# State space convolution moved from VectorE to TensorE: four shifted projections with weights scaled by the taps

## The reference

```python
def _mamba(x, in_proj_w, conv_w, conv_b, x_proj_w, dt_proj_w, dt_proj_b, A_log, D, out_proj_w):
    xz = x @ in_proj_w.T
    xc, z = jnp.split(xz, 2, axis=-1)
    xt = jnp.pad(jnp.moveaxis(xc, 1, 2), ((0, 0), (0, 0), (D_CONV - 1, 0)))
    xt = conv(xt, conv_w, feature_group_count=D_INNER)      # 4 taps, one filter per channel
    xc = _silu(jnp.moveaxis(xt, 1, 2) + conv_b)
    x_dbl = xc @ x_proj_w.T
    dt = softplus(x_dbl[..., :DT_RANK] @ dt_proj_w.T + dt_proj_b)
    ...
    def step(h, ins):                                       # along the 256 rows
        dt_t, B_t, C_t, u_t = ins
        h = h * exp(dt_t[..., None] * A) + (dt_t * u_t)[..., None] * B_t[:, None, :]
        return h, einsum('bdn,bn->bd', h, C_t)
    ...
    y = y + D * xc
    return (y * _silu(z)) @ out_proj_w.T
```

## Time and profile before

| | us |
|---|---|
| median of 3 runs | 1524.51 (1522.3 to 1524.8) |
| the profiled execution | 1535.18 |
| its span in the trace | 1533.7 |

### The profile page before, as it was taken

The page is one execution under the profiler, slowest core; times in us unless marked ns, Lnnn a source line. Parts: engine busy times, 40 slices in busy tenths (PEclk is TensorE's granted clock), DMA queues, the critical chain, the costliest instruction groups (busy, mean ns, idle before and its releaser), DMA issues. The chain is left out here.

```text
span 1533.7 us, 31701 instructions
## 1 busy us (share of the span) xinstructions
PE 1304.3 (85%) x11784; PEld 805.7 (53%) x11784; DVE 1259.5 (82%) x3917; ACT 973.0 (63%) x1505; POOL 418.7 (27%) x316
## 2 busy tenths in 40 slices
PE   7999899998999988999958597678879789567746
PEld 4555566655665655666634484366347446323313
DVE  1355059999999998999999999998997787878983
ACT  6777778888786876878833353266677578434330
POOL 4110012232322213222222321222343343422450
PEclk9999999999998998999979799879979979678767
DMA  7878320333213320330005122104466356223320
GB/s 158 216 189 266 57 32 30 53 57 57 29 29 57 57 32 28 57 53 14 33 23 176 42 78 89 55 29 136 137 170 180 102 139 180 79 59 111 93 74 7
DMA packets 96856, 132.69 MB, mean 87 GB/s; under 512 B 20192, under 2 KB 80872, under 8 KB 93744
## 3 DMA queue, kind: packets, MB, share of 16 engines
q1 hardware_dynamic: 96688, 130.50, 33.6%
HBM read 124.95 MB, written 5.51 MB: 85 GB/s over the span
## 5 line engine op out<-in xcount | busy, mean ns | idle before, releaser
L1434 ACT ACTIVATE attn_arena<-ps 128x1024 f32<-128x1024 f32 x512 | 497.5, 1025 | 142.4 <-PE ps L456 139.6
L2066 DVE MATCH_REPLACE8 attn_late<-attn_shared,attn_late 128x256 f32<-128x256 f32 x1024 | 411.6, 410 | 0.0
L2063 DVE MAX8 attn_shared<-attn_late 128x8 f32<-128x256 f32 x1024 | 381.3, 415 | 11.9 <-ACT attn_late L1460 10.7
L456 PE MATMUL ps<-attn_arena 32*128 32x256 f32 x4096 | 343.0, 407 | 7.8 <-ACT attn_arena L1434 3.2
L470 PE MATMUL ps<-attn_arena 128*32 128x256 f32 x4096 | 279.0, 389 | 6.5 <-ACT attn_early L1442 3.0
L456 PEld LDWEIGHTS ps<-attn_arena 32*128 32x128 f32 x4096 | 231.4, 188 | 92.8 <-issue 65.4
L1297 POOL TENSOR_SCALAR attn_late<-attn_late 128x512 f32<-128x512 f32 x64 | 95.7, 1495 | 595.1 <-DVE attn_late L2066 595.1
L470 PEld LDWEIGHTS ps<-attn_arena 128*32 128x32 f32 x4096 | 109.2, 110 | 138.8 <-issue 63.1
L739 PE MATMUL ps<-attn_arena,attn_q 128*128 128x512 f32 x256 | 134.4, 660 | 15.0 <-DMA attn_arena<-ctxT 15.0
L1310 POOL TENSOR_TENSOR attn_late<-attn_late 128x1024 f32<-128x1024 f32 x48 | 113.2, 2362 | 121.5 <-DVE ps L1889 121.5
L761 PE MATMUL ps<-attn_arena 128*128 128x256 f32 x512 | 128.1, 396 | 0.0
(11 more groups left out here) (249 smaller groups left out, 1622.7 us busy)
## 6 DMA issues: line engine op xcount, KB each, us to landing
attn_arena<-ctxT SPq DMA_DIRECT2D x124, 256.0 KB, 4.7
attn_arena<-ctx SPq DMA_DIRECT2D x32, 512.0 KB, 4.2
attn_late<-rows SPq DMA_DIRECT2D x256, 64.0 KB, 2.3
attn_arena<-ctxV SPq DMA_DIRECT2D x15, 1024.0 KB, 13.0
attn_late<-maskT SPq DMA_DIRECT2D x20, 512.0 KB, 6.6
attn_late<-wide SPq DMA_DIRECT2D x64, 128.0 KB, 2.7
attn_early<-wide SPq DMA_DIRECT2D x64, 128.0 KB, 3.3
attn_arena<-maskT SPq DMA_DIRECT2D x12, 512.0 KB, 11.9
```

Of the source, the lines that this page charges most:

```text
L456: mm = pe.matmul(ps[:, first + j - 2 * i, u * S:(u + 1) * S], kx[n % 2][rows, k0:k0 + P], qpad[rows, n % GROUPS, b * S:(b + 1) * S], start ...
L1434: act.activation(probs[m % 2][:, 2 * i:2 * i + 2], ps[:, first:first + 2, :], ACT.Exp, scale=1.0 / 16.0).then_inc(exp_done, 1)
L2063: dve.max(top[:, t, turn], s[:, i, t] if turn == 0 else work[:, i, t]).then_inc(picked, 1)
L2066: dve.match_replace(work[:, i, t], top[:, t, turn], s[:, i, t] if turn == 0 else work[:, i, t], LOW).then_inc(picked, 1)
```

## The change

The convolution commutes with the projection: the sum over taps n of tap[c, n] times the projection of a shifted input is four projections of shifted inputs with weights scaled by the taps. `xT` gets three zero columns ahead of its 256, the taps are loaded as rows over all partitions into `wtap` (1 MB in place of the 8 KB of `cw`), and POOL multiplies them by the weights once, in step 49. PE then makes xc by four accumulating matmuls for each channel block (`make_xc`), in slot 1 of the step p-4, and z (`make_z`) in slot 2 behind it. ACT's `soften` reads the bank itself, with the bias, in slot 2, and Silu of z and `scale_input` follow in slot 3. DVE's `convolve`, ACT's copy to `xcp` and the semaphore `cv_ready` go. The size of a scratch area for dynamic DMAs is halved, which makes room for `wtap`.

```diff
-        xT = cut(early, 512, 2, S)
-        xcp = cut(early, 2560, C, S + TAPS - 1)
+        xT = cut(early, 512, 2, S + TAPS - 1)
+        xcd = cut(early, 2566, C, S)
+        wtap = sb("wtap", [P, 2, TAPS, C * P])
...
-            def make_xz(name, i):
+            def make_xc(i):
                 d = i % 2
-                if d == 0 and name == "xc":
+                if d == 0:
                     pe.wait_ge(misc_taken, misc["xs", i // 2] + 1)
-                    pe.wait_ge(ssm_loaded, SSM_LOADS)
-                begin(name, "ssm", i)
+                    pe.wait_ge(ssm_consts, 3)
+                    pe.wait_ge(ssm_zeroed, 3)
+                begin("xc", "ssm", i)
                 for k in range(C):
-                    m = k + (C if name == "z" else 0)
-                    mm = pe.matmul(M_[:, k * S:(k + 1) * S], win[:, d, m * P:(m + 1) * P], xT[:, d, :], start=True, stop=True)
+                    for n in range(TAPS):
+                        mm = pe.matmul(M_[:, k * S:(k + 1) * S], wtap[:, d, n, k * P:(k + 1) * P], xT[:, d, n:n + S], start=(n == 0), stop=(n == TAPS - 1))
+                mm.then_inc(misc_made, 1)
+
+            def make_z(i):
+                d = i % 2
+                begin("z", "ssm", i)
+                for k in range(C):
+                    mm = pe.matmul(M_[:, k * S:(k + 1) * S], win[:, d, (C + k) * P:(C + k + 1) * P], xT[:, d, TAPS - 1:], start=True, stop=True)
                 mm.then_inc(misc_made, 1)
...
                         for i in passes(-4, p):
-                            make_xz("z", i)
+                            make_xc(i)
...
                     if slot == 2:
+                        for i in passes(-4, p):
+                            make_z(i)
                         for i in passes(-2, p):
                             start_y(i)
...
                     if slot == 3:
-                        for i in passes(-5, p):
-                            make_xz("xc", i)
...
-            for w, name in ((nw, "nw"), (nb, "nb")):
+            for w, name in ((nw, "nw"), (nb, "nb"), (wtap.rearrange("p d n c -> p (d n c)"), "taps")):
                 sp.dma_start(w, a[name].partition_broadcast(P)).then_inc(ssm_loaded, 16)
...
+                    pool.wait_ge(ssm_loaded, SSM_LOADS)
+                    step(pool.tensor_tensor(wtap[:, 0], wtap[:, 0], win[:, 0, 0:C * P].unsqueeze(1).to_broadcast([P, TAPS, C * P]), ALU.mult))
+                    pool.tensor_tensor(wtap[:, 1], wtap[:, 1], win[:, 1, 0:C * P].unsqueeze(1).to_broadcast([P, TAPS, C * P]), ALU.mult).then_inc(ssm_consts, 1)
...
-                act.wait_ge(cv_ready, i + 1)
+                act.wait_ge(misc_made, misc["xc", "ssm", i] + 1)
                 if i:
                     act.wait_ge(du_ready, i)
-                act.activation(xcs, cvv, ACT.Silu).then_inc(u_ready, 1)
-                act.wait_ge(u_ready, i + 1)
+                act.activation(xcs[:, 0, :], M_[:, 0:S], ACT.Silu, bias=cb[:, d, 0:1])
+                act.activation(xcs[:, 1, :], M_[:, S:2 * S], ACT.Silu, bias=cb[:, d, 1:2]).then_inc(misc_taken, 1)
+                act.wait_ge(misc_taken, misc["xc", "ssm", i] + 1)
+                act.sem_inc(u_ready, 1)
+
+            def scale_input(i):
...
-                            take_misc(xcp[:, :, TAPS - 1:], M_.rearrange("p (c s) -> p c s", c=C), "xc", "ssm", i)
...
                         for i in passes(-4, p):
+                            soften(i)
+                    if slot == 3:
+                        for i in passes(-4, p):
                             act.wait_ge(misc_made, misc["z", "ssm", i] + 1)
                             if i >= 3:
                                 act.wait_ge(gated, i - 2)
                             act.activation(sz[i % 3], M_.rearrange("p (c s) -> p c s", c=C), ACT.Silu).then_inc(misc_taken, 1)
-                    if slot == 3:
-                        for i in passes(-4, p):
-                            soften(i)
+                            scale_input(i)
...
-            def convolve(i):
-                d = i % 2
-                dve.wait_ge(misc_taken, misc["xc", "ssm", i] + 1)
-                dve.wait_ge(ssm_zeroed, 3)
-                for k in range(C):
-                    tap = lambda n: xcp[:, k, n:n + S]
-                    step(dve.tensor_scalar(cvv[:, k, :], tap(TAPS - 1), cw[:, d, k, TAPS - 1:TAPS], cb[:, d, k:k + 1], ALU.mult, ALU.add))
-                    for n in range(TAPS - 1):
-                        ins = dve.scalar_tensor_tensor(out=cvv[:, k, :], in0=tap(n), scalar=cw[:, d, k, n:n + 1], in1=cvv[:, k, :], op0=ALU.mult, op1=ALU.add)
-                        if n < TAPS - 2 or k < C - 1:
-                            step(ins)
-                ins.then_inc(cv_ready, 1)
...
-                if turn == 4:
-                    for i in passes(-4, p):
-                        convolve(i)
...
-    nc = bacc.Bacc("TRN2", target_bir_lowering=False, num_devices=1)
+    nc = bacc.Bacc("TRN2", target_bir_lowering=False, num_devices=1, dynamic_dma_scratch_size=8192)
```

More of the change, by code:

```diff
@@ L246, in attention @@
         A = cut(arena, 23392, 2, 2 * 4, QUADS)
-        cw, cb = cut(arena, 23456, 2, C, TAPS), cut(arena, 23472, 2, C)
+        cb = cut(arena, 23472, 2, C)
         bdt, dcol = cut(arena, 23476, 2, C), cut(arena, 23480, 2, C)
@@ L253, in attention @@
         xs = cut(early, 0, T, E)
-        xT = cut(early, 512, 2, S)
-        gx = cut(early, 1024, 2, C, S)
-        xd = cut(early, 2048, 2, S)
-        xcp = cut(early, 2560, C, S + TAPS - 1)
+        xT = cut(early, 512, 2, S + TAPS - 1)
+        gx = cut(early, 1030, 2, C, S)
+        xd = cut(early, 2054, 2, S)
+        xcd = cut(early, 2566, C, S)
+        wtap = sb("wtap", [P, 2, TAPS, C * P])
         cvv = cut(early, 3078, C, S)
@@ L804, in start_y @@
                 pe.wait_ge(xcd_ready, i + 1)
-                pe.matmul(y_of(i), ident[:], xcp[:, :, TAPS - 1:], start=True, stop=False, skip_group_check=True).then_inc(y_started, 1)
+                pe.matmul(y_of(i), ident[:], xcd, start=True, stop=False, skip_group_check=True).then_inc(y_started, 1)
             def add_states(i, h):
@@ L1128, in _ @@
             sp.wait_ge(pv_done, CROSS_ITS)
-            for w, name in ((win, "win"), (wx, "wx"), (wout, "wout"), (alog, "alog"), (cw, "cw"), (cb, "cb"), (bdt, "bdt"), (dcol, "dcol")):
+            for w, name in ((win, "win"), (wx, "wx"), (wout, "wout"), (alog, "alog"), (cb, "cb"), (bdt, "bdt"), (dcol, "dcol")):
                 sp.dma_start(w, a[name]).then_inc(ssm_loaded, 16)
-            for w, name in ((nw, "nw"), (nb, "nb")):
+            for w, name in ((nw, "nw"), (nb, "nb"), (wtap.rearrange("p d n c -> p (d n c)"), "taps")):
                 sp.dma_start(w, a[name].partition_broadcast(P)).then_inc(ssm_loaded, 16)
@@ L1404, in _ @@
                     pool.tensor_tensor(xs, xs, nb.unsqueeze(1).to_broadcast([P, T, E]), ALU.add).then_inc(xs2_ready, 1)
[L1405 to L1407 removed]
+                if p == SSM_P[0] - 7:
+                    pool.memset(xT[:, :, 0:TAPS - 1], 0.0).then_inc(ssm_zeroed, 1)
                 if p == SSM_P[0]:
@@ L1546, in soften @@
                 d = i % 2
-                act.wait_ge(cv_ready, i + 1)
+                act.wait_ge(misc_made, misc["xc", "ssm", i] + 1)
                 if i:
                     act.wait_ge(du_ready, i)
-                act.activation(xcs, cvv, ACT.Silu).then_inc(u_ready, 1)
-                act.wait_ge(u_ready, i + 1)
+                act.activation(xcs[:, 0, :], M_[:, 0:S], ACT.Silu, bias=cb[:, d, 0:1])
[3 more added lines that the diff above has]
+            def scale_input(i):
+                d = i % 2
+                if i:
+                    act.wait_ge(y_started, i)
                 for k in range(C):
-                    ins = act.activation(xcp[:, k, TAPS - 1:], xcs[:, k, :], ACT.Identity, scale=dcol[:, d, k:k + 1])
+                    ins = act.activation(xcd[:, k, :], xcs[:, k, :], ACT.Identity, scale=dcol[:, d, k:k + 1])
                 ins.then_inc(xcd_ready, 1)
@@ L2136, in layouts @@
         "win": c(np.stack([w.T for w in both(i, "in_proj_w")], 1)),
-        "cw": c(np.stack([w.reshape(C, P, TAPS).transpose(1, 0, 2) for w in both(i, "conv_w")], 1)),
+        "taps": c(np.stack([w.reshape(C * P, TAPS).T for w in both(i, "conv_w")]).reshape(-1)),
         "wx": c(np.stack([np.concatenate([w[RANK:], w[:RANK]]).T.reshape(C, P, -1).transpose(1, 0, 2) for w in both(i, "x_proj_w")], 1)),
```

6 lines of the change are left out of this document (2 added, 4 removed).

## The result

The changed kernel takes **1545.74 us** (median of four runs, 1541.12 to 1551.22), the kernel before 1524.65 us (four runs, 1522.30 to 1526.53): a ratio of **1.0137, interval 1.0105 to 1.0169**, 21 us slower. The forecast was 1535, with 1505 to 1550 as its range. The direction is the forecast's; the size is twice its +10.7 us.

The account below looks back on a forecast made before the run. The bound was taken to change hands between VectorE and TensorE. Terms by step summed to +10.7 us on the profiled 1535.18 us, 1545.9, or 1535 us on the median's scale, with a range of 1505 to 1550.

Parts of the forecast that it names:

- Step 60: Pass 0: TensorE's added +2.5 us nearly covered by its 4.47 us wait for GpSimd; VectorE keeps its saving, -3.5 us.
- Steps 68, 80, 85 and 89: Router's logits, state sums, an FFN product and the output projection, each against VectorE's saving: +4.5, +2.1, -2.1, +1.9 us.
- Step 76: Two context score tiles end 3.5 us later, and VectorE's maximum follows: +2.4 us (0 to 2.5).
- The load: 1 MB of taps ahead of the context keys: 2.8 us at 375 GB/s, about half hidden; +1.5 us (0 to 3).
- Step 64: Context output projection starts 3.5 us later behind xc and z, so VectorE adds it late: +1.4 us (-1 to +3).
- Step 72: VectorE already waited 2.05 us for the context products, with TensorE full before: +2.5 us (0 to 2.5).
- Faster: VectorE stays the bound and bank 7 has slack: whole 31.9 us saving stays, 1494 us, half gives 1509; chance 0.20.
- No change: Context products, context scores and state sums cost nothing, router's logits 2 us: sum +1.2, or 1526 us; chance 0.14.
- A better clock: Added matmuls keep TensorE at 2.4 GHz, 13.8 us of lost time on the path: sum -3.1, 1521 us; chance 0.08.
- Worse: xc starts after a wait at 1.2 GHz, 3.7 us more in six passes: +22 more, 1557 us; chance 0.08.
- rival C: Set up for the follow-up runs: the load and ScalarE's work, laid bare, give VectorE's saving back; no chance given.

Follow-up runs that it names:

- z_four: Kernel before, each product of the z projection made four times over (12 added TensorE instructions a pass, slot 1 of p-4): 1536.32 us, ratio 1.0063.
- before_one_tap: Kernel before, VectorE applying one tap and leaving the other three out of the result: 1520.73 us, ratio 0.9951.
- one_tap: Changed kernel in its own order, only the last tap's product for xc, as many products as before: 1538.24 us, ratio 1.0065.
- z_first: Changed kernel with z projected before xc and copied out, bank 7 handed over at the old times, taps loaded late: 1539.15 us, ratio 1.0074.
- early_xc: Changed kernel with xc's 16 instructions at the old place, slot 3 of p-5, and z in slot 1 of p-4: 1546.45 us, ratio 1.0114.
- the square: Four variants of the change, over before: old handover with one or four products for xc, -0.3 and +12.0 us; late handover, +10.8 and +21.6.
- no_load: Changed kernel without the 1 MB load and GpSimd's two products, taps left out of the result: 1542.63 us, ratio 1.0103.

## Why the prediction was right in direction and wrong in size

The sum came to +10.7, and by the same steps the change costs +20.6. Step 60 makes 4.4 us of the difference, steps 48 and 76 make 2.7 each, steps 64 and 72 1.3 and 1.1.

**The mechanism held.** The removed work is worth little, since TensorE or ScalarE is late next; the saving comes back behind bank 7 and behind TensorE. Steps 68, 80, 85 and 89 were forecast at +4.5, +2.1, -2.1 and +1.9 and came at +3.7, +2.0, -2.3 and +1.7. The price of +2.5 us a pass for 12 more instructions is that of z_four (2.2 to 2.6) where TensorE bounds.

**Step 60 failed: -3.5 forecast, +0.9 measured.** This is the largest miss, 4.4 us. The step looked at one wait only, TensorE's 4.47 us for GpSimd, and let VectorE keep 0.6 to 4.0. Two things were wrong. The wait and the half-clock products behind it were one execution's (2.80 us and full clock in the second profile); 2.8 of the 4.4 us are the difference between the two executions of before in this stretch. And who is late next for VectorE was not asked. The first is ScalarE's copy of the sums, which in the first profile ended at 1024.55, 3.1 us ahead of VectorE's reciprocal at 1027.66, and in the second at 1018.20, 1.4 us ahead of 1019.63. The second is ScalarE's logarithm for pass 0, for which VectorE already waited 3.61 us in the profile that the prediction read (VectorE in the first profile, the second, before_one_tap and the change):

```profile
1050.52 0.69 DVE L1865 SCALAR_TENSOR_TENSOR attn_early<-attn_early 128x512 f32<-128x512 f32 x1 [3.61 <-ACT attn_early L1576]
...
1039.69 0.69 DVE L1865 SCALAR_TENSOR_TENSOR attn_early<-attn_early 128x512 f32<-128x512 f32 x1 [0.80 <-ACT attn_early L1576]
...
1047.97 0.69 DVE L1863 SCALAR_TENSOR_TENSOR attn_early<-attn_early 128x512 f32<-128x512 f32 x1 [2.09 <-ACT attn_early L1576]
...
1044.92 0.69 DVE L1867 SCALAR_TENSOR_TENSOR attn_early<-attn_early 128x512 f32<-128x512 f32 x1 [1.91 <-ACT attn_early L1594]
```

In before_one_tap the copy of the sums takes 1.65 us of the 3.1 saved and the logarithm 2.09 - 0.80 = 1.3, so the removal is worth nothing here even with bank and TensorE as before.

**Step 76: +2.4 forecast, +5.1 measured.** The forecast moved the last context tile by 3.5 us, which holds from the end of the first pair of tiles on. But that pair is late itself (the change's TensorE, then VectorE, beside the earlier trace rows):

```profile
1244.05 6.25 PE L740 MATMUL ps<-attn_arena,attn_q 128*128 128x512 f32 x8 [4.46 <-DMA attn_arena<-ctxT]
1250.13 3.62 PE L784 MATMUL ps<-attn_early,attn_wtap 128*128 128x256 f32 x16
...
1256.89 1.22 DVE L1841 TENSOR_REDUCE attn_mx<-attn_arena 128x1 f32<-128x1024 f32 x1 [7.21 <-ACT attn_arena L1541]
1259.47 1.22 DVE L1841 TENSOR_REDUCE attn_mx<-attn_arena 128x1 f32<-128x1024 f32 x1 [1.36 <-ACT attn_arena L1541]
```

TensorE waits 4.46 us for the keys there and then takes 6.25 us for the pair that took 3.70, partly at half clock (granted clock 0.50 from 1244 to 1247 us). Neither part of the change makes 5.1 alone: the late handover without the added products (one_tap) costs 1.6 us, with a wait of 2.50 and a pair of 5.40, the added products with the old handover (z_first) cost 1.9, with 1.86 and 5.40. It takes both; why the keys are later was not tried apart.

**The load: +1.5 forecast, 0 to 3 as bounds; +4.2 in step 48, of which 0.8 comes back.** Taking the load away gains 3 to 5 us. The 4.2 is in part this execution's: over steps 48 to 59 the three runs with the same instructions there (change, one_tap, early_xc) pay 2.7 to 3.4. The forecast priced the transfer (2.8 us at the full rate, half of it hidden) and left out what follows the longer wait: products at half clock, 2.75 us more in the change and 1.69 in one_tap.

**Step 64: +1.4 forecast, +2.7 measured.** The output projection was looked at; the last attention products, which stand just behind xc on TensorE and which VectorE wants first, were not. VectorE waited 6.5 us for them (line 1891 in the waits above). **Step 72:** the bound of 2.5 was full length of the products; with the handover it is 3.6.

**The scale was no fault, but luck.** The prediction laid its sum on the first profile and scaled by 0.7 %. The two first profiles lie 9.6 us apart, which looks like the forecast's 10.7; against a second profile of before it is 21.5, and from 743 us on it is 20.6, or 15.9 against the first. The 7.3 us by which the first profile was longer ahead of 743 us did no harm, since no term was read there; the 2.8 in step 60 did.

**The rivals.** *Faster* fell: VectorE keeps a quarter of what is taken from it (6.7 of 25 us), and step 68 costs 3.7 where under 2 was the point from which it decides. *No change* fell with it. *A better clock* fell: the stages show 0.85, 0.96 and 0.91. *Worse* fell: xc's instructions have a median of 378 ns and a longest of 483, and 16 of them take 3.62 us, all at full clock. The range of terms (-7 to +24) held the +21.

So of the 21 us, -7 are VectorE's saving (before_one_tap, where a fifth of the work stayed), +3 to +5 the load, and the rest, 23 to 25 by subtraction and 21.9 in the square, TensorE's products and the late handover in near equal parts. Of rival C's two parts the load is the smaller term of the loss; ScalarE's work, laid bare, is seen in step 60, where it keeps VectorE's saving from counting.

## What to carry to other kernels

Work taken from an engine is worth only what lies before its next wait, so for each place ask which engine is late next, and read it from every queue that feeds that instruction, not from one. Work added to an engine costs by what stands behind it in the queue of whoever takes its result: the same 96 instructions cost 9.7 us at one place and 19.7 at another. And a stretch that carries a term of a sum should be read in two executions, since one may have run at half clock there.

## What the runs showed of the hardware

Two things had no price at these places of the sum. A wait has a second price on TensorE: after 6.07 us of waiting for keys the next products took 3.78 and 2.08 us, after 4.69 us (one_tap) 3.67 and 1.13, after 1.92 us (no_load) 1.98 and 1.13. From 820 to 828 us the granted clock of the change was 0.50, its 1.2 GHz level, and that of no_load 1.00, the 2.4 GHz level; in the change it fell between 818 and 820 us, while TensorE was still waiting. And the same place of the same kernel can be at full clock in one execution and not in another: the eight products of step 60 ran at 0.50 in the first profile of before, behind a wait of 4.47 us, and at 1.00 in the second, behind 2.80.

And GpSimd can hold VectorE: 0.41 us became 2.43 and 2.38 beside products of 2.35 and 2.34 us. The Trainium skill, "SBUF — State Buffer", section "SBUF: two separate sides", says that VectorE and GpSimd share a pair of ports as an exclusive lock for a whole instruction, when VectorE's runs in a mode that uses two ports or has two inputs in SBUF beside a GpSimd instruction that reads SBUF; the trace agrees, as GpSimd's instruction began first both times and both VectorE instructions last until its end. In which mode VectorE's two ran is not shown. In step 49 of the change the same two products ran beside VectorE's maxima (lines 2062 and 2065) and reductions (line 1841) and lengthened none of them.
